# Attention in query halves and key-tile pairs, with later heads' projections inside the loop and splits on GpSimd

## The reference

```python
lat = layer_norm(layernorm(x))                  # 1024 x 128
kv_in = concat([layer_norm(ctx), lat])          # 7428 x 128
q, k, v = lat @ Wq, *split(kv_in @ Wkv)         # 16 heads of 64
attn = softmax(q @ k.T * 64 ** -0.5)            # per head 1024 x 7428
x = x + (attn @ v, heads side by side) @ Wout
```

## Time and profile before

| | |
|---|---|
| time, three runs | 2881.78, 2882.93, 2882.50 us; median 2882.5 |
| span of the profiled execution | 2884.0 us (no other time is given for it) |
| busy in it | TensorE 2658.8, VectorE 2348.5, ScalarE 2271.1, GpSimd 55.4 us |
| mean granted TensorE clock | 0.957 of 2.4 GHz |
| first exponential of head 0 | at 175.2 us |
| last exponential of head 15 | at 2494.6 us |

### The profile page before, as it was taken

How to read it: one execution, slowest core, us unless ns; L and a number is a source line. 1 busy time by engine, 2 the same in 40 slices (tenths; PEclk the granted TensorE clock), 3 DMA queues, 4 the chain that set the end, 5 groups by cost and what they waited for, 6 DMA issues and landing times. The chain is left out here.

```text
span 2884.0 us, 93692 instructions
## 1 busy us (share of the span) xinstructions
PE 2658.8 (92%) x35639; PEld 1734.1 (60%) x35639; DVE 2348.5 (81%) x3328; ACT 2271.1 (79%) x2645; POOL 55.4 (2%) x95
## 2 busy tenths in 40 slices
PE   2799999999999999999999999999999999959996
PEld 1256665656565656565656566666656566747884
DVE  8789897979797979798888888888979797547864
ACT  4889897979797979797979798988979795426652
POOL 2100000000000000000000000000000000012001
PEclk9999999999999999999999999999999999979998
DMA  2000000000000000000000000000000000060000
GB/s 75 1 2 1 2 1 2 1 2 1 2 1 1 1 1 1 1 2 1 2 1 2 1 2 0 2 1 2 1 2 0 2 1 2 8 169 1 2 2 10
DMA packets 16345, 22.30 MB, mean 8 GB/s; under 512 B 1960, under 2 KB 13808, under 8 KB 15728
## 3 DMA queue, kind: packets, MB, share of 16 engines
q1 hardware_dynamic: 12816, 14.55, 1.7%
q10 hardware_dynamic: 3296, 4.10, 0.5%
HBM read 18.13 MB, written 0.52 MB: 6 GB/s over the span
## 5 line engine op out<-in xcount | busy, mean ns | idle before, releaser
L800 DVE TENSOR_TENSOR att_prob_low<-att_prob 128x1024 f16<-128x1024 f32 (+1 forms) x944 | 1153.7, 1223 | 196.7 <-ACT att_prob L678 195.9
L678 ACT ACTIVATE att_prob<-all_banks 128x1024 f32<-128x1024 f32 (+1 forms) x944 | 966.0, 1025 | 112.8 <-PE all_banks L565 32.6
L672 ACT ACTIVATE att_scores<-all_banks 128x1024 bf16<-128x1024 f32 x768 | 783.2, 1024 | 0.9 <-PE all_banks L495 0.6
L553 PEld LDWEIGHTS all_banks<-att_v,att_prob 128*128 128x128 bf16 x7552 | 538.3, 99 | 117.5 <-issue 16.1
L553 PE MATMUL all_banks<-att_v,att_prob 128*128 (+1 forms) x7552 | 597.7, 193 | 5.1 <-ACT att_prob L678 5.1
L554 PE MATMUL all_banks<-att_v,att_prob 128*128 (+1 forms) x7552 | 598.5, 195 | 0.0
L554 PEld LDWEIGHTS all_banks<-att_v,att_prob 128*128 128x128 bf16 x7552 | 506.0, 98 | 101.6
L535 PE MATMUL all_banks<-att_qc,att_kc 128*128 (+1 forms) x1888 | 562.5, 379 | 0.0
L535 PE MATMUL all_banks<-att_qd,att_kd 128*128 (+1 forms) x1888 | 562.0, 379 | 0.0
L495 PE MATMUL all_banks<-att_kc,att_qc 128*128 (+1 forms) x1792 | 534.3, 380 | 19.0 <-ACT att_scores L672 14.2
L774 DVE TENSOR_TENSOR att_running<-att_running,att_scores 128x1024 bf16<-128x1024 bf16 x768 | 525.9, 685 | 13.9 <-ACT att_scores L672 13.5
(11 more groups left out here) (276 smaller groups left out, 2810.3 us busy)
## 6 DMA issues: line engine op xcount, KB each, us to landing
prep_ctx<-in_ctx SPq DMA_DIRECT2D x5, 640.0 KB, 8.6
later_ctx<-in_ctx SPq DMA_DIRECT2D x1, 3200.0 KB
experts_up<-in_L_ffn_f SPq DMA_DIRECT2D x1, 2048.0 KB, 8.3
prep_wkv<-in_L_xattn_Wkv ACTq DMA_DIRECT2D x1, 1024.0 KB, 12.3
all_X<-in_x SPq DMA_DIRECT2D x1, 512.0 KB, 4.5
prep_wq<-in_L_xattn_Wq ACTq DMA_DIRECT2D x1, 512.0 KB, 14.5
wout_w<-in_L_xattn_Wout SPq DMA_DIRECT2D x1, 512.0 KB, 4.1
out<-all_X SPq DMA_DIRECT2D x2, 256.0 KB, 2.5
```

What stands on the lines that cost most here:

```text
L553: pe.matmul(O[:, j // 4, o:o + DH + 1], w, high, start=False, stop=False, skip_group_check=True)
L672: act.activation(o[:, :], banks[:, :, :].rearrange("p a q -> p (a q)"), ACT.Copy).then_inc(max_copied, 1)
L678: act.activation(prob[t % 2][0:n, :], S[t % 2][0:n, :], ACT.Exp, scale=SCALE).then_inc(exp_done, 1)
L800: dve.tensor_tensor(prob_low[t % 2][0:n, :], p, p.bitcast(BF16)[:, 1:2 * TOKENS:2], op=ALU.subtract)\
```

## The change

The constants and the whole of stage_attention's order change.

- A **unit** g is two key tiles by 512 queries. A head has two halves of 30 units (29 pairs and the tail), UNITS = 60. O is one bank for a half, and normalize_half runs twice a head. One Fori runs over pairs of heads, fully unrolled inside: 7 iterations, then heads 14 and 15.
- **Projections** leave the space between heads. V of head b+1 is made in the first half of head b, after the units V_AT; K of head b+2 in the second half, after the units K_AT, each through the one bank Y. Q of head b+2 comes at unit 58.
- **Maxima:** of a query tile's seven slots, 0, 2 and 4 (COPIED) go through ScalarE and merge as before. Slots 1, 3, 5, 6 (DIRECT) are reduced by VectorE straight from the PSUM pair X. There is one running tile.
- **Splits** of units whose slot is direct (32 of 60) run on GpSimd. prob_low has three buffers.
- Head 0: K and Q, then all slots on X alone, with V of head 0 and K of head 1 between them.

```diff
-BODY = 14
+HALF = TOKENS // 2
+PAIRS = FULL_TILES // 2
+UNITS = 2 * (PAIRS + 1)
...
+        COPIED = (0, 2, 4)
+        DIRECT = (1, 3, 5, 6)
+        V_AT = (1, 5, 8, 12, 15, 19, 22, 26)
+        K_AT = (1, 3, 5, 6, 8, 10, 12, 15, 17, 19, 20, 22, 24, 26, PAIRS - 1)
+        REST_AT = {PAIRS - 1: (0, 1), PAIRS: (2, 3)}
...
+        def by_pool(g):
+            slot = slot_of(g)
+            return slot is not None and slot % MAX_CHUNKS in DIRECT
```

The order of a head on GpSimd:

```diff
+            def head(b, e):
+                for g in range(UNITS):
+                    if by_pool(g):
+                        pool.wait_ge(exp_done, EXP0 + b * UNITS + g + 1)
+                        pool.wait_ge(low_done, LOW0 + b * UNITS + g - 2)
+                        p = prob[g % NP][:, :]
+                        pool.tensor_tensor(prob_low[g % NL][:, :], p, p.bitcast(BF16)[:, 1:4 * BANK:2],
+                                           op=ALU.subtract).then_inc(split_pool, 1)
```

The order of a head on TensorE:

```diff
+            def head(b, e, with_max, with_keys):
+                for g in range(UNITS):
+                    h, p = divmod(g, SIDE)
+                    if g == 0:
+                        pe.wait_ge(v_split, (b + 1) * V_GROUPS)
+                    apply_high(b, e, g)
                     if with_max:
+                        if slot_of(g) is not None:
+                            max_slot(b + 1, 1 - e, slot_of(g))
+                        elif h == 0:
+                            rest_step(b + 1, 1 - e, REST_AT[p][0])
+                    if p:
+                        apply_low(b, e, g - 1)
+                    if p == PAIRS:
+                        apply_low(b, e, g)
+                    if with_max and h == 0 and p in REST_AT:
+                        rest_step(b + 1, 1 - e, REST_AT[p][1])
+                    if with_max and h == 0 and p in V_AT:
+                        project_v(b + 1, V_AT.index(p))
+                    if with_keys and h == 1 and p in K_AT:
+                        project_keys(b, K_AT.index(p))
+                    if with_max and g == LAST - 1:
+                        pe.wait_ge(exp_done, EXP0 + b * UNITS + g + 1)
+                        spread_top(b + 1, 1 - e)
+                        if with_keys:
+                            wait_slot_read(pe, b + 1, MAX_SLOTS - 1)
+                            project_q(b + 2, 0)
+                            project_q(b + 2, 1)
+                    if g + 2 < UNITS:
+                        score(b, e, g + 2)
+                    elif with_max and g == LAST:
+                        score(b + 1, 1 - e, 0)
+                        score(b + 1, 1 - e, 1)
...
+            def exp(b, g):
+                act.wait_ge(scored, b * UNITS + g + 1)
+                act.wait_ge(high_done, HIGH0 + b * UNITS + g - 1)
+                wait_split(act, *((b, g - 2) if g >= 2 else (b - 1, g - 2 + UNITS)))
```

The order of a head on ScalarE:

```diff
+            def head(b, e, with_max, with_keys):
+                for g in range(UNITS):
+                    h, p = divmod(g, SIDE)
+                    if g + 1 < UNITS:
+                        exp(b, g + 1)
                     if with_max:
+                        if slot_of(g) is not None and slot_of(g) % MAX_CHUNKS in COPIED:
+                            copy_slot(b + 1, slot_of(g))
+                        if h == 0 and p in V_AT:
+                            copy_v(b + 1, 1 - e, V_AT.index(p))
+                    if with_keys and h == 1 and p in K_AT:
+                        copy_keys(b + 2, e, K_AT.index(p), Y)
...
+            def take_direct(m, slot):
+                j, c = tile_chunk(slot)
+                dve.wait_ge(max_scored, m * MAX_SLOTS + slot + 1)
+                dve.tensor_reduce(part[:, j, DIRECT.index(c):DIRECT.index(c) + 1], X[:, :, :], axis=AX.XY, op=ALU.max)\
+                   .then_inc(direct_taken, 1)
...
+            def maxima(m, g):
+                slot = slot_of(g)
+                if slot is not None and slot % MAX_CHUNKS in DIRECT:
+                    take_direct(m, slot)
+                if g and slot_of(g - 1) is not None and slot_of(g - 1) % MAX_CHUNKS in COPIED[1:]:
+                    merge(m, slot_of(g - 1))
+                if slot is not None and slot % MAX_CHUNKS == COPIED[-1] + 1:
+                    fold(m, slot // MAX_CHUNKS)
```

The order of a head on VectorE:

```diff
+            def head(b, e, with_max, with_keys):
+                for g in range(UNITS):
+                    h, p = divmod(g, SIDE)
+                    if with_max and g == LAST - 1:
+                        finish_max(b + 1)
+                    if not by_pool(g):
+                        split(b, g)
                     if with_max:
+                        maxima(b + 1, g)
+                        if h == 0 and p in REST_AT:
+                            rest_step(b + 1, REST_AT[p][0])
+                    if p == PAIRS:
+                        normalize_half(b, h)
+                    if with_max and h == 0 and p in REST_AT:
+                        rest_step(b + 1, REST_AT[p][1])
+                    if g:
+                        projected(b, e, g - 1, with_max, with_keys)
+                if with_keys:
+                    split_q(b + 2, e, 0)
+                    split_q(b + 2, e, 1)
```

More of the change, by code:

```diff
@@ L372, in kwidth @@
             return min(BANK, KEYS - c * BANK)
-        def bank(c):
-            return S[1 - c % 4 // 2][:, (c % 2) * BANK:(c % 2) * BANK + kwidth(c)]
         def group(g):
             return list(range(8 * g, min(8 * g + 8, KEY_TILES)))
[L381 to L407, removed]
@@ new lines, in apply_low @@
+            def apply_low(b, e, g):
+                wait_split(pe, b, g)
+                for i, t in tiles(g):
+                    for q in range(4):
+                        w = prob_low[g % NL][:, i * BANK + q * P:i * BANK + (q + 1) * P]
+                        o = q * (DH + 1)
+                        last = pe.matmul(O[:, o:o + DH + 1], w, v[:, e, t, 0:DH + 1], start=False, stop=True,
+                                         skip_group_check=True)
+                last.then_inc(low_done, 1)
@@ new lines, in _ @@
+            act.wait_ge(constants, 1)
+            act.activation(warm[:, :], zeros[0:1, 0:1], ACT.Exp).then_inc(exp_done, EXP0)
+            for c in range(K_CHUNKS):
+                copy_keys(0, 0, c, pers.banks[:, c % 4, :])
+            copy_q(0, 0, 0)
+            copy_q(0, 0, 1)
+            for g in range(UNITS):
+                h, p = divmod(g, SIDE)
+                if slot_of(g) is not None and slot_of(g) % MAX_CHUNKS in COPIED:
+                    copy_slot(0, slot_of(g))
+                if h == 0 and p in V_AT:
+                    copy_v(0, 0, V_AT.index(p))
+                if h == 1 and p in K_AT:
+                    copy_keys(1, 1, K_AT.index(p), Y)
@@ new lines, in merge, with fold @@
+            def merge(m, slot):
+                j, c = tile_chunk(slot)
+                n = merge_index(j, c)
+                dve.wait_ge(max_copied, m * copies_before(MAX_SLOTS) + copies_before(slot + 1))
+                if COPIED.index(c) > 1:
+                    dve.wait_ge(merged, MERGED0 + m * MERGES + n)
+                r = running[:, :]
+                dve.tensor_tensor(r, r, scores16[n % 2][:, :], op=ALU.max).then_inc(merged, 1)
+            def fold(m, j):
+                r = running
+                dve.wait_ge(merged, MERGED0 + m * MERGES + (j + 1) * (len(COPIED) - 1))
+                dve.tensor_tensor(r[:, 0:BANK], r[:, 0:BANK], r[:, BANK:2 * BANK], op=ALU.max).then_inc(part_done, 1)
+                dve.wait_ge(part_done, m * TOKEN_TILES + j + 1)
+                dve.tensor_reduce(part[:, j, 4:5], r[:, 0:BANK], axis=AX.X, op=ALU.max).then_inc(folded, 1)
@@ L832, in normalize_head @@
[L832 to L843 removed]
+                dve.wait_ge(direct_taken, (m + 1) * (MAX_SLOTS - copies_before(MAX_SLOTS)))
```

625 lines of the change are left out of this document (267 added, 358 removed).

## The result

The changed kernel takes 3107.2 us, median of four runs (3101.5 to 3111.6), against 2882.1 us for the kernel before beside it: a ratio of 1.078, 95% interval 1.0766 to 1.0796. The forecast was 3143 us.

A forecast was written before the change was run, and what follows sets the result against it. TensorE was taken as the limit in the loop, with gain on offer between heads. Start, stalled heads, jumps, last heads and the untouched rest summed to 3144 us, forecast as 3143; own range 3040 to 3220, 8-in-10 range 2890 to 3260.

The forecast's parts named there:

- the start: From 68 us to head 0's first exponential: 142 us, with all 56 slots one after another on X.
- head 15: Last head, only exponentials and splits: VectorE and GpSimd splits excluding each other make it 105 us instead of 93.6.
- Work of a head: TensorE's own work per head if nothing stalls: 138.3 us, against 150.3 us a head before.
- Head as such: One head without a jump back: 138.3 us of work plus 22.2 of stalls, 160.5 us.
- The order on which most hung: At a tile's end, GpSimd split 6 blocks merge 4, delaying direct read 6; TensorE stands 2.0 us in the first half.
- K at unit 6: Second half, two of four tiles: the K product waits for a K split behind direct read 6, 3.45 us each.
- order alone: Rival: GpSimd's splits and VectorE's operations do not block each other; 145.5 us a head, 2910 us in all; chance 0.12.
- The shared access: Likeliest case: VectorE operations with two SBUF inputs and GpSimd's splits exclude each other, stalling TensorE; 3143 us, chance 0.58.
- GpSimd waits too: Assumed that GpSimd's split also waits for VectorE's operation; without that wait a head is about 157 us, not 160.5.
- Jumps: Loop jumps back, 6 instead of 13, at 7 us each: 42 us.
- the clock falls: Rival: two 3.45 us waits a head drop TensorE's clock, 6.6 us a head, 24 in the start; 3260 us, chance 0.10.
- TensorE never waits: Rival: merge and fold fit in gaps, no stalls; 138.3 us a head, 2799 us in all; chance 0.20.

The follow-up runs named there:

- the version that runs at clock 1.00: Kernel with five copied slots, even K, head 0's maxima on two PSUM pairs and later folds, plus Q and first rest moved earlier: 2847.1 us, ratio 0.9881.
- the last two versions: Five copied slots, even K, later folds, Q and first rest moved earlier: 2847.1 us with 16 GpSimd splits a head; 2834.7 us (one run) with none.
- The two pairs: Changed kernel with head 0's maxima alternating between X and the second score pair, instead of X alone: 3051.9 us, one run.
- the later 16: GpSimd's splits per head with two direct slots of seven; removed from the 2847.1 us kernel with reordered Q and rests, the time was 2834.7 us, one run.

## Why the prediction came out as it did

**The sum.** The terms against the windows: the start 142, measured 159.1; fourteen heads with jumps 2247 + 42 = 2289, measured 2253.4 (227.1 to 2480.5); head 14 151, 148.6; head 15 105, 94.1; the rest 389, 386.6. The differences, +17, -36, -2, -11 and -2, add to -34, and the time lies 36 below the forecast.

**Work of a head.** 138.3 forecast; 140.0 in the version that runs at clock 1.00. In heads 4 and 5 of the changed kernel it is 142.3 and 143.6, at a clock of 0.99 and 0.98, which is 1.6 to 3.2 us of 160.

**Direct read.** 1.22 forecast, 1.222 measured. **GpSimd split** 2.1 forecast, mean 1.97, with 1.89 where nothing is beside it.

**Head as such.** 160.5 forecast, about 160.0 without a jump. That agreement is partly luck, because two errors cancel. In head 5 (159.9 us) TensorE is idle 16.3 us where the stalls were to be 22.2, and busy 143.6 where 138.3 was forecast. Of the 5.3 us more, 1.7 is work and the rest goes with the clock. Of the 5.9 us less, about 3 are the direct reads of the first half: 8.2 forecast, 3.3 found in three tiles and 1.8 ahead of the first rest for the fourth.

**The order on which most hung** (GpSimd split 6, merge 4, direct read 6) is there, with the merge blocked, and taking GpSimd's reads away took the stall away. Its price was wrong: 2.0 us expected at the maxima product, 0.9 to 1.1 found, since merge 4 starts 0.8 us into GpSimd's 1.89 and is held for 0.95, where the hand-worked timeline held it for nearly a whole split. Head 15 was made too long by the size of a split: at 1.88 (60.28 / 32) seven units hold the shared access 3 x 1.2 + 4 x 1.88 = 11.1 us, inside TensorE's 11.2. K at unit 6 was to wait 3.45 and waits 2.8 to 2.9. In the version without GpSimd's reads it waits 1.9, as the rival "order alone" had it (1.85). That rival gave 145.5 a head and 2910 in all; with the reads away heads are 147.5 and the time 2932.

**The shared access** was named the mechanism, and the run without GpSimd's reads bears it out. It is not the whole account. With no GpSimd splits at all the time is the same, so what holds the changed kernel up is VectorE's queue at a tile's end, whether blocking or a split fills it. The prediction gave "order alone" as what is left without blocking, and did not see that giving the splits back fills the same place.

**GpSimd waits too**: yes. Here is GpSimd, and under it VectorE, in head 2:

```profile
549.89 2.62 POOL L442 TENSOR_TENSOR att_prob_low<-att_prob 128x1024 f16<-128x1024 f32 x1 [13.69 <-ACT att_prob L683]
```

```profile
549.53 1.23 DVE L795 TENSOR_TENSOR att_prob_low<-att_prob 128x1024 f16<-128x1024 f32 x1 [1.96 <-issue]
```

Its 2.62 us are the 0.87 left of VectorE's split and then 1.75, about its own 1.89.

**Jumps** were to cost 7 us. Heads behind a jump take 162.5 on average against 160.0, and TensorE's issue waits are 1.8 to 3.3 where the earlier trace rows had 3.7. They are of two kinds: heads 4, 6 and 8 take 160.5 to 161.1, heads 2, 10 and 12 take 164.0 to 164.5. In the long ones the granted clock is 0.96 to 0.97, in the others 0.98 to 0.99. In the run with all splits on VectorE heads behind a jump are no longer than the rest (160.4 and 160.6 on average).

**The start** was 17 us low. Slots one after another were right; that the clock would be at 1.2 GHz for most of it had been put aside as "up to 24 more". The two pairs show what one pair cost: 48 us, half of it by the clock.

**The rival "the clock falls"** was to cost 6.6 us a head, by falls behind the two waits for K at unit 6. A clock below 1.00 inside the heads was named as its sign, and the clock is 0.96 to 0.99 there. But it falls mostly elsewhere. The windows below are, in head 5, behind the waits of 1.8 and 1.4 us for the rests between the halves, and behind the second K wait of 2.8; in head 2, behind the first K wait of 2.8:

```profile
1101.00:1111.00 10.00, 8.27 (x67) 4.85 (x68) 6.55 (x12) 2.50 (x3) 0.29 (x1) 0.66 0.00 1
1165.00:1171.00 6.00, 6.00 (x70) 3.52 (x71) 3.07 (x4) 4.05 (x5) 1.90 (x1) 1.00 0.01 3
643.80:649.80 6.00, 6.00 (x55) 3.50 (x56) 1.70 (x2) 3.25 (x4) 1.89 (x1) 0.72 0.01 3
```

In 5 us slices of the trace it falls at the rests in every head from 1 to 13. In head 5 that is about 3.4 us of lost clock ((1 - 0.66) x 10). Behind a K wait it falls in heads 2, 7, 10, 11 and 12 only, although these waits are equally long in all heads. The three long heads behind a jump are among them.

**"TensorE never waits"** did not happen here, but the last two versions come near it with the prediction's own work term: 145 a head, of which 140 is work. It put its point of decision at 143.6 a head with a start of 142; with the start of 105.5 that the last two versions have, and 15 us of jumps, the same formula gives 148.1, and 145 is enough.

What stays open: why the clock falls behind a K wait of 2.8 us in some heads and not in others; what the third low buffer is worth; and what placing the rests elsewhere would give, which was not tried.

## What to carry to other kernels

When work is interleaved by hand, sum what each engine has in each unit, not over the loop: here 1.1 us in one unit of seven was worth 69 us, on an engine that was idle a quarter of the time. Work given to an idle engine gains only if the engine that loses it had it on a path that something waits for, and only what the two do not take from each other. The 32 splits a head on GpSimd were worth 171 us and cost 175 by blocking; the later 16 filled time that VectorE had free, and gained nothing. And one buffer between a producer and a reader that take nearly the whole unit gives every lateness on, and in the start it cost the clock as well.

## What the runs showed of the hardware

The blocking is of one instruction by about the rest of another, in both directions: a VectorE merge of 0.68 us took 1.63 with 1.08 left of GpSimd's split, and a GpSimd split of 1.89 took 2.62 with 0.87 left of VectorE's. A GpSimd instruction that only writes (the memset of 1.79 us) blocked no merge, and reductions from PSUM were never blocked (at most 1.227 us). A GpSimd subtract of f32 and every second bf16, 128x1024, took 1.89 us, less than the 2.12 of f32 and f16 in the earlier trace rows. And the reductions from PSUM of 1024 elements at 1.222 us cost as much as a split of the same size.
